# Query bias and query parts moved to the Pool engine in an expert stage, with the bias row loaded for each tile and the stack products two places later

## The reference, cut to what matters

```python
def _expert(x, Wqkv, bqkv, Wo, bo, g1, be1, W1, bf1, W2, bf2, g2, be2):
    qkv = x @ Wqkv.T + bqkv
    q, k, v = jnp.split(qkv, 3, axis=-1)
    ...
    attn = jax.nn.softmax(jnp.einsum('bhqd,bhkd->bhqk', q * scale, k), axis=-1)
    ...
    x = _layernorm(x + ctx, g1, be1)
    h = jax.nn.gelu(x @ W1.T + bf1, approximate=False)
    h = jax.nn.gelu(h @ W2.T + bf2, approximate=False)
    return _layernorm(x + h, g2, be2)
```

## Time and profile before

| | us |
|---|---|
| median of 3 runs | 3311.03 |
| lowest and highest | 3310.53, 3320.87 |
| the profiled execution, its own time | 3312.79 |
| its span in the profile | 3311.0 |

### The profile page before, as it was taken

How to read it: one execution, slowest core, us unless ns; L and a number is a source line. 1 busy time by engine, 2 the same in 40 slices (tenths; PEclk the granted TensorE clock), 3 DMA queues, 4 the chain that set the end, 5 groups by cost and what they waited for, 6 DMA issues and landing times.

```text
span 3311.0 us, 66796 instructions
## 1 busy us (share of the span) xinstructions
PE 2771.7 (84%) x24695; PEld 1945.2 (59%) x24695; DVE 1838.1 (56%) x4886; ACT 1884.5 (57%) x4218; POOL 545.7 (16%) x728
## 2 busy tenths in 40 slices
PE   7788785999998999899989937798789878987898
PEld 5456454567666666566656623465565556565676
DVE  4664665676766676677666621344444444444454
ACT  2232233678776777687767738377347634853343
POOL 2000003243234323442132220000000000000000
PEclk9986887899999999999999968799899979998999
DMA  5000006766676665667555510100000000000000
GB/s 205 1 10 29 1 10 218 229 205 187 200 212 181 208 193 182 191 220 203 149 161 142 161 57 1 44 1 1 13 10 1 1 14 5 1 1 13 6 1 5
DMA packets 162466, 304.09 MB, mean 92 GB/s; under 512 B 19729, under 2 KB 121226, under 8 KB 154442
## 3 DMA queue, kind: packets, MB, share of 16 engines
q1 hardware_dynamic: 158818, 293.69, 29.0%
q0 software_dynamic: 3328, 6.14, 0.7%
HBM read 227.00 MB, written 72.75 MB: 91 GB/s over the span
## 4 chain that ended last, share of the span: by engine, by line
PE 50%; DVE 14%; issue 12%; ACT 9%; DMA 4%; DVEq 3%; POOL 3%; POOLq 2%; PEld 1%; ACTq 1%; PEldq 1%; SPq 0%
PE ps L1835 5%; PE ps L1500 4%; PE ps L1518 4%; PE ps L1479 4%; DMA xg<-slots_x 3%; PE ps L1313 3%; PE ps L1967 2%; PE ps L1767 2%; PE ps L1543 2%; PE ps L1929 2%; PE ps L1905 2%; PE ps L1552 2%; PE ps L1298 1%; DVE peaks L2640 1%; POOL wts L1163 1%
## 5 line engine op out<-in xcount | busy, mean ns | idle before, releaser
L2640 DVE TENSOR_REDUCE peaks<-ps 128x1 f32<-128x748 f32 x608 | 556.9, 932 | 267.9 <-PE ps L1479 250.7
L2148 ACT ACTIVATE pt<-ps 128x384 f32<-128x384 f32 x1216 | 562.2, 491 | 193.7 <-PE ps L1500 178.5
L1500 PE MATMUL ps<-qst,kst 98*128 98x128 bf16 x3648 | 392.4, 224 | 14.9 <-ACT pt L2148 9.8
L1500 PEld LDWEIGHTS ps<-qst,kst 98*128 98x128 bf16 x3648 | 244.4, 99 | 171.5 <-ACT pt L2148 56.6
L1133 POOL TENSOR_TENSOR rstd<-var,minus_half 128x6 f32<-128x6 f32 x40 | 53.0, 1324 | 1725.5 <-DVE var L2890 1277.5
L1479 PE MATMUL ps<-kst,qst 96*128 96x374 bf16 x1216 | 305.1, 333 | 10.3 <-DVE peaks L2640 6.2
L1518 PE MATMUL ps<-pt,vst 128*32 128x128 f32 (+1 forms) x7296 | 273.0, 282 | 0.1
L1518 PEld LDWEIGHTS ps<-pt,vst 128*32 128x32 f32 (+1 forms) x7296 | 188.4, 111 | 89.3 <-issue 60.0
L1479 PEld LDWEIGHTS ps<-kst,qst 96*128 96x128 bf16 x1216 | 99.9, 100 | 24.0 <-DVE peaks L2640 9.1
L2718 DVE CAST qst<-ps 96x1024 bf16<-96x1024 f32 x76 | 92.7, 1219 | 34.1 <-PE ps L1430 33.2
L1929 PE MATMUL ps<-k_stack,q_stack 128*128 128x374 f32 (+5 forms) x256 | 90.2, 456 | 9.5 <-ACT parts L2345 6.1
(11 more groups left out here) (657 smaller groups left out, 6538.9 us busy)
## 6 DMA issues: line engine op xcount, KB each, us to landing
kst<-saved_k SPq DMA_DIRECT2D x76, 1176.0 KB
wf<-in_l SPq DMA_DIRECT2D x76, 512.0 KB
saved_k<-kparts SPq DMA_DIRECT2D x168, 192.0 KB, 3.3
vst<-saved_v SPq DMA_DIRECT2D x76, 408.0 KB, 3.3
saved_v<-vprod SPq DMA_DIRECT2D x32, 408.0 KB, 3.3
rows<-in_l_rows SPq DMA_DIRECT2D x76, 128.0 KB
slots_x<-zeros SPq DMA_DIRECT2D x4, 1216.0 KB, 11.3
wq<-in_l SPq DMA_DIRECT2D x76, 64.0 KB, 2.9
```

Of the source, the lines that this page charges most:

```text
L1500: mm = pe.matmul(out[:, c * P:(c + 1) * P], kst[0:STACK + SHIFT, m % 3, head, j * P:(j + 1) * P], qst[0:STACK + SHIFT, m % 3, head, :], st ...
L2148: act.activation(pt[:, u % (2 * GROUP), :], entry()[:, 0:H0], ACT.Exp, scale=float(HD) ** -0.5)\
L2640: v.tensor_reduce(peaks[:, g, head:head + 1], entry()[:, :, 0:T // 2], XY, ALU.max)\
```

## The change

The bias is no longer added by PE. The table `bq` is saved once to DRAM; for each tile SP loads the owner's row of it, repeated on all 128 partitions, into `bq_rows` (two buffers) ahead of `wq`, and for that waits until Pool has made the parts of the tile that used the buffer before. ACT makes only the fp32 copy. Pool adds the bias row to it, makes the three copies of the first part itself, and goes on as before. The step `stack` moves from u = 7 to u = 9.

```diff
@@ opening_steps
         yield "save_kv", 0, e
+        if e == 1:
+            yield "save_bq",
@@ turn_steps
         put(3, ("query", early))
-        put(7, ("stack", early))
+        put(9, ("stack", early))
@@ buffers
+        bq_rows = sb("bq_rows", [P, 2, P])
...
+        saved_bq = nc.dram_tensor("saved_bq", (E, P), F32).ap()
@@ SP, load_wq(m)
                     if m >= 2:
                         sp.wait_ge(S["ring_done"], made["query", m - 2])
                     e = owner_of(m)
+                    if m >= 2:
+                        sp.wait_ge(S["parts_ready"], m - 1)
+                    if m == 0:
+                        sp.wait_ge(S["bq_saved"], 16)
+                    sp.dma_start(bq_rows[:, m % 2, :], saved_bq[bass.ds(e, 1), :].broadcast_to([P, P]))\
+                        .then_inc(S[f"wq_loaded{m % 2}"], 16)
                     sp.dma_start(wq[:, m % 2, 0:P], A["l1"][bass.ds(e, 1), :, W1_Q:W1_Q + P].rearrange("o p n -> (o p) n"))\
                         .then_inc(S[f"wq_loaded{m % 2}"], 16)
@@ SP, the steps
+                    elif what == "save_bq":
+                        sp.wait_ge(S["tables_loaded"], 64)
+                        sp.dma_start(saved_bq[:, :], bq[0:E, :]).then_inc(S["bq_saved"], 16)
@@ Pool, "query"
+                        pool.wait_ge(S[f"wq_loaded{m % 2}"], n.take(f"wq_loaded{m % 2}", 32))
                         pool.wait_ge(S["rounded_ready"], n.take("rounded_ready"))
+                        pool.tensor_tensor(own, own, bq_rows[:, m % 2, :].rearrange("p (d h) -> p h d", h=E), ALU.add)
+                        pool.drain()
+                        pool.tensor_copy(parts[:, :, 0:3, :], own.unsqueeze(2).to_broadcast([P, E, 3, HD]))
+                        pool.drain()
                         pool.tensor_tensor(own, own, parts[:, :, 0, :], ALU.subtract)
@@ PE, query(m)
-                    pe.wait_ge(S[f"wq_loaded{m % 2}"], n.take(f"wq_loaded{m % 2}", 16))
+                    pe.wait_ge(S[f"wq_loaded{m % 2}"], n.take(f"wq_loaded{m % 2}", 32))
                     pe.wait_ge(S["ring_done"], made["x", m])
                     out = bank()[:, 0:P]
-                    pe.matmul(out, xgT[:, m % 2, :], wq[:, m % 2, :], start=True, stop=False)
-                    pe.matmul(out, onehot[0:E, m:m + 1].to_broadcast([E, P]), bq[0:E, :], start=False, stop=True)\
-                        .then_inc(S["ring_ready"], 1)
+                    pe.matmul(out, xgT[:, m % 2, :], wq[:, m % 2, :], start=True, stop=True).then_inc(S["ring_ready"], 1)
@@ ACT, query(m)
                     src = entry()[:, 0:P].rearrange("p (d h) -> p h d", h=E)
-                    act.activation(qs[:, m % 2, :, 0:3, :], src.unsqueeze(2).to_broadcast([P, E, 3, HD]), ACT.Copy)
                     act.activation(q_own[:, m % 2, :, :], src, ACT.Copy).then_inc(S["ring_done"], 1)
                     act.drain().then_inc(S["rounded_ready"], 1)
```

More of the change, by code:

```diff
@@ L100 @@
     "xs_loaded", "ramps_ready", "ranked", "routed",
-    "scattered", "gathered", "y_stored", "ffn_loaded", "rows_filled", "tables_loaded", "k_split", "k_split_v", "sum_ready",
+    "scattered", "gathered", "y_stored", "ffn_loaded", "rows_filled", "tables_loaded", "bq_saved", "k_split", "k_split_v", "sum_ready",
     "rounded_ready", "parts_ready", "peak_ready", "peak_done", "shift_split", "ring_ready", "ring_done",
```

## The result

| | before | after |
|---|---|---|
| median of 4 runs each, us | 3311.68 | 3353.51 |
| lowest and highest | 3310.53, 3320.87 | 3348.72, 3360.69 |
| the profiled execution, its own time | 3312.79 | 3350.41 |
| its granted clock, mean | 0.920 | 0.905 |

The changed kernel is slower: ratio 1.0122, 95% interval 1.0095 to 1.0149. The forecast was 3351. In the stage the sum came out; its terms did not all come out singly.

The account below looks back on a forecast made before the run. PE was taken to bound the expert stage, with the late x load ending turns behind norm2. Terms: -20 (PE) + 39 (SP) + 15 (clock) + 4 (stack) = +38 us on 3312.79, so 3351 us; range 3312 to 3380.

Parts of the forecast that it names:

- What bounds the kernel: Expert stage, 76 turns: PE sets the pace, except behind norm2, where the late x load ends the turn, 14 times.
- SP's delay: SP's queue in norm2 turns: wq issued 2.6 us later, x landing 2.8 us later, 14 times, 39 us (28 to 48).
- The clock: Behind lengthened x waits: lower granted clock costs 1.7 us each, nine times, 15 us (0 to 21).
- The nine short ones: PE's x waits of 1.6 us or less, among 14: each would grow to over 3 us and pay 1.7 us.
- Removed from PE and ACT: Bias matmul and an ACT activation gone: PE-bound turns 0.42 us shorter, 48 savings, 20 us (16 to 40).
- Added to Pool: An add and a 384-column cast ahead of Pool's old chain: 1.22 us together, between 1.12 and 1.53.
- The rival in which Pool sets the pace: Bare turns wait 0.5 us each at the stack, another 25 us on the forecast, 3376 us; chance 0.08.
- the lock's price: Pool and DVE locking each other out at DVE's cast of peaks: nothing in the sum, 0 to 6 us in range.
- Stack waits: PE's stack waiting for Pool: 21.5 us stay or grow a little; five uncovered turns cost 4 us (0 to 10).
- The sum: Whole kernel: all terms together +38 us against the profiled execution's 3312.79 us, giving 3351 us; chance 0.66.
- the transfer would be hidden: Rival: SP's delay does not reach the x load, leaving PE's savings, 3297 us down to 3275; chance 0.13.
- Half the delay with the clock held: Rival: part of the x delay is taken up and waits stay short, 3317 to 3323 us; chance 0.13.

Follow-up runs that it names:

- wait_only: The kernel before with only SP's wait for Pool's parts added ahead of wq, no row loaded: 3325.08 us, ratio 1.0041.
- four_rows: The changed kernel with four bias-row buffers instead of two, so SP waits for a tile two turns back: 3299.4 us, ratio 0.9957.
- four_stack7: four_rows with the stack moved back from place 9 to its old place 7: 3334.08 us, ratio 1.0071.

## Why the prediction was right, and where its terms were not

**What bounds the kernel, and SP's delay: right.** In the norm2 turns wq is issued 2.9 us later for 2.6 (3.5 in those without saves), and PE's turning of x comes 3.0 us later for 2.8, so 14 x 3.0 = 42 us for the 39; the turns behind norm2 took it up without slack (wait_only 1.0 us of x for 1.3 of wq, four_rows back to +0.7). Norm2 and the turn behind it together lost 49.3 us, where the terms make some 54 (39 + 15 for the clock, and under 1 net for what the three uncovered turns save and wait).

**The clock: too high.** "The nine short ones would grow to over 3 us" failed. The x waits of the 14 turns grew by 1.0 us each (19.7 to 34.0 us), not by 2.8, and of the seven short ones among them only two came to over 3 us (3.1 and 5.6), since PE now comes late to the wait itself, held at the stack (1.9 us before in these turns, 13.3 after) and running at the lower clock there. For the same reason "a sum near 60 us" for all x waits was too high, 46.4. Behind the x waits the low clock took 18.5 us for 9.9 before (each stretch's length times what its clock is under 1), 8.6 us more for the 15. Ahead of them it took another 14.8, for nothing before, but that is covered by the x wait behind it. That the 49.3 us are near the terms comes of this too: the delay was 3 us over its term and the clock at least 6 under.

**Removed from PE and ACT: mis-sized by half.** "PE-bound turns get 0.42 us shorter", with "a further 0.1 us" from ACT of which none was taken, and bare turns of 12.9 to 13.0 us. Measured 12.67, and 21.3 us over the 32 burst and third turns, 0.67 each. The product alone gave 0.30, less than the pitch of 0.42 us promised; the rest came from the two edits costed at nothing, the stack's place (0.13 alone) and what is left over (0.27, ACT's dropped activation or its interplay with the stack's place). By what means was not shown.

**Added to Pool: nearly right.** The cast took 0.50 us as interpolated, the add 0.52; from the start of the add to that of the first subtraction it is 1.31 us (1069.48 to 1070.79), for 1.22. The rival in which Pool sets the pace did not come: in the turn from 1885.45 the stack does not wait. four_stack7 shows it was near, since it comes true two places earlier. DVE's 152 casts of the peaks took 1249 ns at worst after and 40.3 us in all, 1475 ns and 45.4 us before, so nothing is seen of the lock's price that was put into the range.

**Stack waits: too low.** "They stay or grow a little" from 21.5 us; they were 51.9 in 28. "Most of that is covered" held in the changed kernel, where PE still waits for x in each of the 14 turns behind norm2. It does not hold without SP's wait: in four_rows the stack waits are 49.8 us, PE comes to x after it has landed in seven of the 14 turns, and norm2 and the turn behind it together are still 9.4 us longer than before. Even so four_rows is faster in all. What was not covered shows in the gather turns, 5.9 us lost where the terms make 1 us saved (nine savings of 0.42, three waits of 0.9), and part of the cause is Pool's first drain behind a scatter or gather, told of below.

**The range.** "With each term moved half-way to its ends" gives 3326 to 3366 us, not 3325 to 3375; the stated range is wider than both.

**The sum.** The stage's turns came to +35.0 us and the profiled executions to +37.6, for +38. That the sum is within 1 us is luck, since errors of both signs met: 8 us more saved in burst and third turns and 5 less lost around norm2, against 7 more lost in gather turns, 2 in the opening and 3 outside the stage.

**The rivals.** That the transfer would be hidden is refuted by wait_only: the DMA engines are at 0.90 to 0.99 of their time and do not catch up. Half the delay with the clock held would have needed a clock near 1.00 behind norm2.

## What to carry to other kernels

A wait that is added on the queue that issues transfers costs whatever stands behind it, so look at that queue in the turn where it has no gap: the same edit cost 1.2% with the wait ahead of the heavy loads, and gained 0.4% with twice the buffers or 0.9% with the wait behind them. Work moved off a bound engine can gain more than its own instruction (here 0.70 us of a bare turn for a pitch of 0.42), but only in the turns in which nothing else ends last; count the turns by kind. And when one load is late, ask what stands beside it in the queue before moving it.

## What the runs showed of the hardware

**A drain on Pool behind an indirect DMA waits for that DMA.** Pool in the turn behind norm2, after, and the scatter's time from issue to landing (1070 to 1092 us):

```profile
1078.75 1.08 POOL L1166 DMA_INDIRECT slots_x<-xsc,slot_at  x1 [0.18 <-issue]
1082.72 0.51 POOL L1190 TENSOR_TENSOR q_own<-q_own,bq_rows 128x128 f32<-128x128 f32 x1 [2.89 <-ACTq L2137]
1086.32 0.50 POOL L1192 CAST qs<-q_own 128x384 bf16<-128x384 f32 x1 [3.09 <-issue]
...
slots_x<-xsc,slot_at POOLq DMA_INDIRECT x1, 7.4
```

Issued at 1078.75, landed 7.4 us later at 1086.15; the cast behind the drain starts at 1086.32 and not at 1083.4. PE's stack waited 2.5 us for it. In each of the two traces six chains have a scatter ahead of them that lands behind the end of their first operation, and in all twelve the next operation starts 0.15 or 0.16 us after the landing. Of the 76 chains 31 have an indirect DMA as Pool's last instruction ahead of them; before, 12 of these had a gap of 0.95 us or more at the drain, up to 4.66, and after 13, up to 6.44. No chain without one had more than 0.43. The first operation starts freely behind the DMA, only the first drain is held. By the Trainium skill (DMA: Bandwidth & Descriptors, section "Issuing engines are not separate DMA queues") the transfers of all issuing engines run on the same 16 DMA engines; the trace agrees, with 7.4 us for a scatter beside SP's loads and 2.3 us for the same scatter at 693.3, where the DMA engines were at 0.09 of their time.

**Issuing gets slower when the DMA engines are full.** In the turns after, twelve steps of six `saved_k` came behind 3 us in which the DMA engines were at 0.12 of their time or less, and took SP 3.16 to 4.19 us (median 3.4); twelve came behind engines at 0.98 or more and took 3.73 to 5.35 (median 4.2). In the longest, at 1081.11, single ones took 0.46 to 1.75 us.
